# A four-layer graph network kernel: four PSUM banks for the first eight transposed tiles of each attention, reciprocals two at a time, and six small moves

## The reference, cut to what matters

```python
# layer 0: dense attention with a bias matrix made of the edges
bias = full((n, n), NEG); bias[diag, diag] = 0; bias[dst, src] = edge_weight
q, k, v = split(x @ Wqkv.T + bqkv)                       # 8 heads of 64
attn = softmax(q k^T / 8 + bias)                         # 8 x 512 x 512
out = (attn v) @ Wo.T + bo
h = layer_norm(x + out, g1, beta1)
h = layer_norm(h + (h @ W1.T + b1), g2, beta2)
x = layernorm(x + h)
# layer 1: x = layernorm(x + relu(D^-1/2 (A) D^-1/2 (x @ W) + b))
# layer 2: messages of 4 relations, mean over the neighbours, norm, gelu feed-forward, norm
# layer 3: attention over the edges (as counts: the logarithm of a count is added to the score)
a = segment_softmax(q[dst] . k[src] / 8) applied to v[src];  o = a @ Wo
x3 = layer_norm(h + o);  out = layer_norm(x3 + relu(x3 @ W1 + b1) @ W2 + b2)
x = layernorm(x + out)
```

## Time and profile before

| | |
|---|---|
| median of 3 runs | 533.22 us (532.39 to 536.17) |
| the profiled execution, its own time | 533.68 us |
| its span, first to last instruction | 531.8 us |
| TensorE's mean granted clock, share of full | 0.988 |
| busy: TensorE, weight loads, VectorE, ScalarE, GpSimd | 505.5, 345.6, 383.2, 225.3, 278.2 us |

### The profile page before, as it was taken

The page is one execution under the profiler, slowest core; times in us unless marked ns, Lnnn a source line. Parts: engine busy times, 40 slices in busy tenths (PEclk is TensorE's granted clock), DMA queues, the critical chain, the costliest instruction groups (busy, mean ns, idle before and its releaser), DMA issues.

```text
span 531.8 us, 7860 instructions
## 1 busy us (share of the span) xinstructions
PE 505.5 (95%) x2483; PEld 345.6 (65%) x2498; DVE 383.2 (72%) x972; ACT 225.3 (42%) x474; POOL 278.2 (52%) x283
## 2 busy tenths in 40 slices
PE   8999999999998899999999999999999999899992
PEld 3444444445885554787778888889888786565771
DVE  6999987999986786977644863764348625776587
ACT  2102360004615775656451234435525125776365
POOL 5877777677404989303551544523541753876101
PEclk9999999999999999999999999999999998999997
DMA  5823310000393521140862663422453853100002
GB/s 191 317 109 108 112 28 1 0 0 2 92 354 109 156 82 61 40 139 20 258 161 82 182 207 118 124 79 80 130 185 90 251 166 78 51 1 1 2 0 79
DMA packets 32409, 56.48 MB, mean 106 GB/s; under 512 B 5152, under 2 KB 8686, under 8 KB 31864
## 3 DMA queue, kind: packets, MB, share of 16 engines
q1 hardware_dynamic: 19420, 31.61, 19.6%
q0 software_dynamic: 11728, 18.92, 11.9%
q10 hardware_dynamic: 1228, 5.54, 2.7%
HBM read 51.79 MB, written 4.26 MB: 105 GB/s over the span
## 4 chain that ended last, share of the span: by engine, by line
PE 70%; DVE 14%; POOL 6%; ACT 5%; issue 4%; DMA 1%; DVEq 0%; SPq 0%; POOLq 0%; ACTq 0%
PE bank L587 15%; PE bank L564 11%; PE bank L566 11%; PE bank L565 11%; PE bank L693 4%; PE bank L680 3%; PE bank L784 3%; PE bank L783 3%; POOL sp L404 2%; POOL wl L390 2%; DVE hot L1302 2%; DVE hot L1301 2%; PE bank L671 2%; PE bank L645 1%; DVE x L1238 1%
## 5 line engine op out<-in xcount | busy, mean ns | idle before, releaser
L390 POOL TENSOR_TENSOR wl<-wraw,wh 128x512 fp32r<-128x512 f32 (+1 forms) x78 | 101.5, 1317 | 69.8 <-DMA wh<-w 15.4
L587 PE MATMUL bank<-hot 128*128 128x512 bf16 x514 | 114.7, 380 | 2.6 <-DVE hot L1302 1.6
L587 PEld LDWEIGHTS bank<-hot 128*128 128x128 bf16 x528 | 51.2, 98 | 66.2 <-DVE hot L1302 5.2
L445 POOL DMA_INDIRECT edge_bias<-ew,cell_at x68 | 71.5, 1052 | 30.5 <-issue 19.4
L564 PE MATMUL bank<-wh,tl 128*128 128x512 f32 x176 | 69.5, 395 | 0.1
L566 PE MATMUL bank<-wh,th 128*128 128x512 f32 x176 | 68.8, 391 | 0.0
L565 PE MATMUL bank<-wl,th 128*128 128x512 f32 x176 | 68.7, 390 | 0.0
L1302 DVE TENSOR_SCALAR hot<-iota,pair_dst,digit 128x1024 bf16<-128x1024 f16 x68 | 44.3, 651 | 0.2 <-issue 0.2
L955 ACT ACTIVATE sp<-sp,peak 128x512 f32<-128x512 f32 x44 | 31.8, 724 | 23.8 <-DVE peak L1478 23.6
L1283 DVE SCALAR_TENSOR_TENSOR eq<-keyb,key,later 128x384 f16<-128x384 f16 (+1 forms) x68 | 41.2, 628 | 0.1
L1301 DVE TENSOR_SCALAR hot<-iota,ef 128x512 bf16<-128x512 f16 x68 | 33.9, 499 | 6.5 <-PE bank L587 5.4
(11 more groups left out here) (239 smaller groups left out, 1066.3 us busy)
## 6 DMA issues: line engine op xcount, KB each, us to landing
wraw<-w SPq DMA_DIRECT2D x26, 256.0 KB
wh<-w POOLq DMA_DIRECT2D x6, 1024.0 KB, 6.2
keyb<-edge_keys ACTq DMA_DIRECT2D x4, 1088.0 KB, 10.6
wh<-w_rel POOLq DMA_DIRECT2D x4, 1024.0 KB, 5.7
wraw<-w_rel SPq DMA_DIRECT2D x16, 256.0 KB
wraw<-w_qkv SPq DMA_DIRECT2D x8, 256.0 KB
wh<-w_o POOLq DMA_DIRECT2D x2, 1024.0 KB, 7.2
count_rows<-counts SPq DMA_DIRECT2D x1, 2048.0 KB, 14.4
```

The source lines that it names most:

```text
L390: pool.tensor_tensor(wl[n % WSLOTS][:, k, 0:width], wraw[:, q % 3, 0:width], wh[n % WSLOTS][:, k, 0:width], ALU.subtract).then_inc(s["w_lo ...
L445: pool.indirect_dma_start(out=bias_dram, out_offset=bass.IndirectOffsetOnAxis(ap=cell_at[:, c:c + 1], axis=0), in_=ew[:, c:c + 1], in_offs ...
L587: mm = pe.matmul(ps(name)[:], hot[:, slot, 0, i * P:(i + 1) * P], hot[:, slot, 1 + kind, :], start=False, stop=last, skip_group_check=True)
```

## The change

Eight edits of banks, order and queue; the arithmetic stays as it was:

1. Tiles 0 to 7 of the transposed probabilities go through banks 4 to 7 in turn; from tile 8 on three banks again.
2. VectorE takes the reciprocals of two tiles in one instruction of 128 x 2, after a wait for both exponentials. The pair 4b, 4b+1 comes after the peak of tile 4b+2, the pair 4b+2, 4b+3 at the head of the next batch.
3. The load of `iota` is issued by ScalarE's queue, as its first instruction, and no longer by SyncE's.
4. In `f3` the bias matmuls of two tiles stand ahead of both products.
5. Layer 0's first norm: `affine` of tile 0 moves ahead of `centre` of tile 1, and `call_low(3)` behind `centred` of tile 1.
6. Layer 1: `turned(1, 0)` moves ahead of `relu_and_add(2)`.
7. The last norms: `centred(8, 2)` moves behind `centre(8, 3)` and `inverse_root(9, 1)`.
8. There too `affine_and_add(8, 2)` moves ahead of `centred(8, 3)`.

```diff
     def attention(a):
         for m in range(ITEMS):
             use(("score", a, m), m % 4)
-            use(("probT", a, m), 4 + m % 3)
+            use(("probT", a, m), 4 + (m % 4 if m < 8 else (m - 8) % 3))
...
             eng.dma_start(ei[:], edges.rearrange("a p c -> p a c")).then_inc(s["ld_edge"], 16)
-            eng.dma_start(iota[:], iota_d.to_broadcast([P, 2 * N])).then_inc(s["ld_iota"], 16)
             eng.dma_start(er[:], edge_rows.rearrange("a c p -> c a p")).then_inc(s["ld_rows"], 16)
...
+                bias(("f3", 2 * part), 0)
+                bias(("f3", 2 * part + 1), 0)
                 for i in (2 * part, 2 * part + 1):
                     name, tile = ("f3", i), slice(i * P, (i + 1) * P)
-                    bias(name, 0)
                     finish(product(name, lambda k: (hidh[:, k, tile], hidl[:, k, tile]), w_tile(20), 2, start=False,
...
+            act.dma_start(iota[:], iota_d.to_broadcast([P, 2 * N])).then_inc(s["ld_iota"], 16)
             act.wait_ge(s["row_keys"], 1)
...
-                def inverse_of(t):
+                def inverses_of(t):
 
                     c = base + t
-                    dve.wait_ge(s["exped"], c + 1)
-                    dve.reciprocal(scale[:, c:c + 1], total[:, c:c + 1]).then_inc(s["inverse"], 1)
+                    dve.wait_ge(s["exped"], c + 2)
+                    dve.reciprocal(scale[:, c:c + 2], total[:, c:c + 2]).then_inc(s["inverse"], 2)
...
                 for b in range(BATCHES + 1):
                     if b:
-                        inverse_of(4 * b - 1)
+                        inverses_of(4 * b - 2)
                     if b < BATCHES:
                         peak_of(4 * b)
...
                     if b:
                         odd_row(4 * b - 3)
                     if b < BATCHES:
-                        inverse_of(4 * b)
                         peak_of(4 * b + 2)
-                        inverse_of(4 * b + 1)
+                        inverses_of(4 * b)
                     if b:
                         odd_row(4 * b - 1)
                     if b < BATCHES:
                         peak_of(4 * b + 3)
-                        inverse_of(4 * b + 2)
...
             call_low(2)
-            call_low(3)
+            affine(0, 0, 3)
             centre(0, 1, ("o0", 1), x[:, 1, :])
             centred(0, 1, 2)
-            affine(0, 0, 3)
+            call_low(3)
             centre(0, 2, ("o0", 2), x[:, 2, :])
...
             shift_of(3, 1)
+            turned(1, 0)
             relu_and_add(2)
-            turned(1, 0)
             relu_and_add(3)
...
             centre(8, 2, ("f3", 2), h[:, 2, :])
             inverse_root(9, 0)
-            centred(8, 2, 0)
             centre(8, 3, ("f3", 3), h[:, 3, :])
             inverse_root(9, 1)
+            centred(8, 2, 0)
+            affine_and_add(8, 2)
             centred(8, 3, 0)
-            affine_and_add(8, 2)
             affine_and_add(8, 3)
```

## The result

The kernel with the change takes 536.62 us in the median of 7 runs (535.49 to 537.95), beside 534.42 us for 7 runs of the kernel before (532.39 to 536.17). The ratio of the runs is 1.0058, with a 95% interval of 1.0037 to 1.0079: 3.1 us slower (2.0 to 4.2), where +0.9 had been forecast; the two medians themselves lie 2.2 us apart. Measured a second time, beside some of the parts, the same kernel gave 1.0039 (1.0018 to 1.0059), 2.1 us slower, with medians 2.8 us apart. So the loss is known to about 1 us.

A forecast was written before the change was run, and what follows sets the result against it. TensorE, busy 505.5 of 531.8 us, was taken to bound the kernel, with GpSimd in the chain in layer 0's attention. Terms -0.45 + 0 + 3.2 - 0.75 - 1.25 + 0.17 = +0.9 gave a median of 534.1 us, range 530.5 to 536.8.

The forecast's parts named there:

- The pairs, "the loop keeps its length": Attentions: paired reciprocals leave the VectorE and ScalarE loop at 5.12 us but release GpSimd later; +3.2 us, bounds 0 to +4.5.
- the walk through GpSimd: Row-by-row count of GpSimd's scalings and low parts after late reciprocals: layer 0's attention 2.0 us longer, layer 3's 1.2.
- The front, -0.45: Kernel start: iota issued from ScalarE's queue lets the first one-hot tile start 0.45 us earlier; bounds -0.7 to 0.
- so it is carried on: From the start to later stages: the 0.45 us gained is kept, as VectorE leads first and TensorE later.
- The banks, 0: Attentions: the fourth bank removes TensorE's waits at tiles 3 and 7 but gains 0; bounds -2.6 us to 0.
- the tie at 170.82: Layer 0's attention: TensorE's transposes of tile 3 end at 170.82 as VectorE reaches their copy; only one path is cut.
- Layer 0's norm, -0.75: First norm of layer 0: earlier affine of tile 0 removes TensorE's wait before the transposes; -0.75 us, bounds -0.75 to 0.
- Layer 2's start, -1.25: Start of layer 2: moving VectorE's low part ahead frees self2's bank, so self2 of tile 0 starts earlier; -1.25 us.
- The end, +0.17: Last stage: the first f3 tile ends one bias matmul later, VectorE's reordering gives 0; +0.17 us, bounds -0.3 to +0.3.
- Pairs free: Rival, attentions: GpSimd catches up within each batch, so pairs cost nothing; 530.9 us, chance 0.25 (0.07 with the banks' gain).
- Small moves without gain: Rival, layer 0's norm and layer 2's start: each released TensorE runs early into another wait; 536.1 us, chance 0.13.
- The clock: Rival, layer 0's attention: a longer wait before tile 11 lowers TensorE's clock, costing up to 3.4 us; 537.5 us, chance 0.10.

The follow-up runs named there:

- e13: Kernel before with paired reciprocals only for tiles 0 to 15 of each attention, single ones from tile 16: ratio 1.0019 (0.9999 to 1.0039).
- e2: Kernel before with only the load of iota moved to ScalarE's queue: ratio 1.0002 (0.9989 to 1.0016), +0.1 us.
- e5: Kernel before with only the fourth bank for tiles 0 to 7 of the transposed probabilities: ratio 0.9978 (0.9958 to 0.9999).
- e1: The whole change with the load of iota back on SyncE's queue, against the kernel before: ratio 1.0048 (1.0030 to 1.0066).
- e11: The whole change measured once more, against the kernel before: ratio 1.0039 (1.0018 to 1.0059), +2.1 us.
- e3: Kernel before with only the reciprocals taken two at a time: ratio 1.0087 (1.0059 to 1.0115), +4.6 us.
- e4: Kernel before with only the moves in layer 0's first norm and of turned(1, 0): ratio 0.9976 (0.9958 to 0.9994).
- e15: e4 measured again, the two small moves alone against the kernel before: 532.17 us, ratio 0.9978 (0.9960 to 0.9997).
- e8: Kernel before with the two loads exchanged, ei on ScalarE's queue and SyncE's beginning with iota: ratio 1.0003 (0.9981 to 1.0024).
- e10: e4 with the fourth bank, against the kernel before: 529.73 us, ratio 0.9948 (0.9926 to 0.9969).
- e16: e4 with the fourth bank, same kernel as e10, against the kernel before: 532.00 us, ratio 0.9979 (0.9955 to 1.0002).

## Why the prediction was wrong

The sign was right, the size was not: +0.9 was forecast, +2.1 and +3.1 came. The measured 536.62 lies inside the range, close to its upper end. The sum of the parts by the traces is 1.2 above the forecast: 0.7 from the pairs, 0.45 from the front, 0.15 from layer 2's start, less 0.1 from the other terms.

- *The pairs, "the loop keeps its length"*: the step that failed. The prediction counted which operations stand in the loop and found the same ones; it didn't allow that the one it changed could start later. The loop measures 5.28 and not 5.12. Over the three loops of batches 1 to 3 this is 0.47, and it adds to the walk through GpSimd: tile 11 came 1.09 late, where 0.68 was worked out. In layer 0 the first half of the tiles cost 1.39 (e13) where the walk had 1.07, in layer 3 0.74 where it had 0.3. The second half was nearly right: 0.91 against 2.0 - 1.07 = 0.93, and 0.76 against 0.1 and the one scaling of 0.77. Of the 0.91, 0.54 is there at the last peak, where the walk had 0.6 from tile 27. In all 3.9 for 3.2.
- *The front, -0.45*: the second step that failed. The bounds were -0.7 to 0, and the reason given for the lower gain (both transfers slow each other) was treated as a loss of the gain, not as a loss. Against before, `ei` took 1.7 to 2.4 longer to land in the four profiles with `iota` issued beside it, so the first tile started 1.0 to 1.7 later. And then "so it is carried on" failed as well, to the good: e2's time stayed. What came is 0 (+0.1, -0.6 to +0.9) and not -0.45. The Trainium skill, "DMA: Bandwidth & Descriptors", section "Issuing engines are not separate DMA queues", had said that such loads interleave and that only issue time is saved; the trace agrees in that `ei` is slower beside `iota`, and the landing at 5.13 instead of 3.10 shows that a small load with a large one beside it can lose far more than the issue time.
- *The banks, 0*: right by the traces, and for the reason given. With TensorE's side of the tie at 170.82 cut, the peaks stayed where they were to 0.02 us and the batches 5.11 apart (e5).
- *Layer 0's norm, -0.75*: right, -0.80. *Layer 2's start, -1.25*: about -1.1. *The end, +0.17*: from output product to the last instruction it takes 34.11 to 34.14 with the edits (after, e1, e11) and 34.02 to 34.06 without, +0.1.
- *The rivals.* Pairs free: refuted by e3. Small moves without gain: its 536.1 is nearest to the measured 536.6, but its mechanism is refuted by e4; the gain came, and the pairs took more. The clock: not in the profile of after, where the granted clock was 1.00 from 164 to 216 us though TensorE stood 1.26 us before tile 11's transposes. But in e1 it did fall there, behind the shorter stand of 0.71, and cost 0.6 to 0.7 us (53.37 against 52.70 to 52.75). So this rival came in one of the four profiles with all the pairs (after, e1, e3, e11); it can't carry the loss.

The clock's price, 3.4 us, was too high as well. Windows (length, busy time of each engine, granted clock, DMA share, GB/s) of e4 and of e15, which are one and the same kernel:

```profile
446.00:454.00 8.00, 6.46 (x45) 4.51 (x45) 6.46 (x23) 6.05 (x16) 6.14 (x10) 1.00 0.05 17
```
```profile
446.00:454.00 8.00, 8.00 (x41) 6.25 (x40) 5.08 (x18) 4.76 (x13) 5.14 (x7) 0.62 0.06 17
```

With the clock at 0.62 attention 3 took 493.03 - 440.85 = 52.18 us, without the fall 50.58; in the profile of before, with 0.57, it took 52.19. In e8, e10 and e16, where the clock in this window was 0.79 to 0.82, it took 51.4. So the fall costs 0.8 to 1.6 us, not the 3.4 taken from the window: in that stretch TensorE has stands which the slower matmuls fill (busy for 8.00 us here, 6.46 without the fall).

## What to carry to other kernels

Merging two small instructions off the critical path saved nothing here, while the first result of each pair comes later; look at who is waiting for it, and walk that engine's queue in its order (here GpSimd's, with a low part between the two scalings). When a walk says that a loop keeps its length, its steps have to be the same operations in the same form: 0.08 at a wait that is met twice in each batch was 0.47 us after three batches. And a wait in the list that a freed bank will remove is worth nothing where the next wait of the same engine ends at the same moment: compare the two times before counting it.

## What the runs showed of the hardware

- A load of 102 KB (`ei`) landed 2.1 to 2.6 us after its issue began when the load of 256 KB (`iota`) came 0.5 behind it on the same queue (11 profiles), and 4.0 to 4.7 after it when both began at 0.8 from two queues (5 profiles), whichever queue took which.
- VectorE's reciprocal of two columns began 0.06 to 0.07 us later behind the same exponential than that of one column (0.90 to 0.92 and 0.83 to 0.86 after the exponential's start).
- The peaks of attention 0 lie at the same places to 0.05 us in the ten profiles with single reciprocals, on different chips, while the stretch from 5 to 130 us differs by up to 3 us between profiles with the same front. Lengths within a stage resolve 0.1 us, at the same granted clock, where medians of 10 runs resolve 1.
- TensorE's granted clock fell in one execution of a kernel and not in another. In e4 and e15, the same kernel, the second scores of attention 3 had stood 0.78 and these 0.21 us before they started, to the hundredth in both:

```profile
445.87 0.50 PE L671 MATMUL bank<-kh,ql 64*128 64x512 f32 x1 [0.21 <-DVE peak L1478]
```
```profile
445.62 0.79 PE L671 MATMUL bank<-kh,ql 64*128 64x512 f32 x1 [0.21 <-DVE peak L1478]
```

  The first ran at 2.4 GHz, the second at 1.2, the lower of the two levels. So a profile with a fall and one without it differ by 0.6 to 1.6 us for no reason that lies in the change. The Trainium skill, "TensorE: Matmul & The Clock Gate", Part 1, says that the moment at which the clock switches varies between runs of one kernel; here a fall came in one execution and not in the other.
